# A conditioned residual block with a gathered layer norm: y begun a batch ahead, h read ahead of x^T, gathers issued later, batch 1's statistics taken before the nets

## What is computed

```python
h = ln(x, pw_g[path], pw_b[path]); h = ln(h, cp_g[cls], cp_b[cls])
t = ln(x, tm_g[cls], tm_b[cls]);   s = ln(x, ms_g[scale], ms_b[scale])
m, n, r = [x + mlp_ln(state_i) for the three states]     # one row per batch
cat = [w0*h, w1*t, w2*m, w3*n, w4*r, w5*s]               # w = softmax(aw)
out = x + ln(silu(cat @ W1 + b1) @ W2 + b2) * g + be
```

## Time and profile before

| | us |
|---|---|
| median of three runs (lowest, highest) | 998.59 (990.33, 999.7) |
| the profiled execution | 992.41 |
| its span, first to last instruction | 990.7 |
| PE busy in the span | 956.3 |
| DVE busy | 802.9 |
| POOL busy | 455.5 |
| PE idle for DVE's `ts_mult` (12 times) and `h_low` (8 times) | 12.3 and 7.1 |

### The profile page before, as it was taken

One profiled execution on the slowest core, in us unless ns is written; L12 is line 12 of the kernel. 1 busy time (PEld: TensorE's weight loads), 2 busy tenths in 40 slices (PEclk: granted clock), 3 DMA queues, 4 the chain that ended last, 5 costly groups with the idle time before them and its releaser, 6 DMA issues. The chain is left out here.

```text
span 990.7 us, 13506 instructions
## 1 busy us (share of the span) xinstructions
PE 956.3 (97%) x4196; PEld 773.7 (78%) x4196; DVE 802.9 (81%) x1183; ACT 271.4 (27%) x341; POOL 455.5 (46%) x619
## 2 busy tenths in 40 slices
PE   7999998999999999999999999999999999999997
PEld 6677877778877787887888888777877878787885
DVE  6887969788696878979787896978869697896965
ACT  4532232231322213223231322223132222313211
POOL 3335244445443554445455444545544355454322
PEclk9999999999999999999999999999999999999999
DMA  9956363847548465563847456384664838466362
GB/s 312 324 215 192 103 196 117 244 105 238 149 141 228 137 209 131 174 198 119 262 139 225 125 184 187 119 249 126 217 146 145 238 117 242 97 211 171 96 149 64
DMA packets 97425, 174.33 MB, mean 176 GB/s; under 512 B 10216, under 2 KB 48872, under 8 KB 93440
## 3 DMA queue, kind: packets, MB, share of 16 engines
q1 hardware_dynamic: 74432, 108.04, 33.8%
q0 software_dynamic: 22976, 66.07, 25.0%
HBM read 141.33 MB, written 32.75 MB: 176 GB/s over the span
## 5 line engine op out<-in xcount | busy, mean ns | idle before, releaser
L1440 PE MATMUL hid_ps<-cat_hi,w_hi 128*128 128x512 f32 x1008 | 394.1, 391 | 7.5 <-DVE cat_lo L961 7.1
L1441 PE MATMUL hid_ps<-cat_lo,w_hi 128*128 128x512 f32 x1008 | 392.5, 389 | 0.0
L1442 PE MATMUL hid_ps<-cat_hi,w_lo 128*128 128x512 f32 x1008 | 392.4, 389 | 0.0
L1440 PEld LDWEIGHTS hid_ps<-cat_hi,w_hi 128*128 128x128 f32 x1008 | 189.2, 188 | 53.3 <-DVE cat_lo L961 11.3
L1442 PEld LDWEIGHTS hid_ps<-cat_hi,w_lo 128*128 128x128 f32 x1008 | 189.2, 188 | 39.7
L1441 PEld LDWEIGHTS hid_ps<-cat_lo,w_hi 128*128 128x128 f32 x1008 | 189.3, 188 | 38.9
L555 POOL DMA_INDIRECT pw_rows<-cp,class_now x64 | 103.0, 1610 | 162.5 <-DVE y_sb L969 152.3
L734 ACT ACTIVATE cat_hi<-v_ring 128x1024 fp32r<-128x1024 f32 x64 | 67.9, 1062 | 335.5 <-DVE v_ring L951 335.4
L548 POOL DMA_INDIRECT pw_rows<-pw,path_now x64 | 75.5, 1179 | 83.6 <-DVE y_sb L994 71.4
L569 POOL DMA_DIRECT2D r_sb<-x x60 | 57.6, 959 | 108.0 <-DVE r_sb L1056 99.6
L1537 PE MATMUL o_ps<-w_hi,hid_hi 128*128 128x512 f32 x240 | 93.4, 389 | 0.0
(11 more groups left out here) (170 smaller groups left out, 1209.2 us busy)
## 6 DMA issues: line engine op xcount, KB each, us to landing
x_sb<-xp SPq DMA_DIRECT2D x16, 1024.0 KB, 4.8
out<-r_sb SPq DMA_DIRECT2D x64, 256.0 KB, 4.0
xc<-xT SPq DMA_DIRECT2D x15, 1024.0 KB, 10.2
h_turned<-y_sb SPq DMA_DIRECT2D x60, 256.0 KB, 6.4
r_sb<-x POOLq DMA_DIRECT2D x60, 256.0 KB, 5.4
v_ring<-h_turned SPq DMA_DIRECT2D x60, 256.0 KB, 4.1
stats_bc<-token_stats SPq DMA_DIRECT2D x30, 256.0 KB, 5.5
ids_sb<-ids SPq DMA_DIRECT2D x16, 256.0 KB, 5.8
```

The source lines that it names most:

```text
L1440: pe.matmul(acc, w1_hi[:, k, cols], hi, start=start, stop=False)
L1441: pe.matmul(acc, w1_hi[:, k, cols], lo, start=False, stop=False)
L1442: return pe.matmul(acc, w1_lo[:, k, cols], hi, start=False, stop=stop)
```

## The change

The matmuls and the vector instructions stay the same. What moves is their order.

On SP, `h_read(b, 0)` comes before `load_xT(b + 1)`:

```diff
-                if not by_pe(b):
+                if not first:
                     h_write(b)
+                    h_read(b, 0)
                 if not (first or last):
                     load_xT(b + 1)
-                if not by_pe(b):
-                    h_read(b, 0)
+                if not first:
                     h_read(b, 1)
-                if not first:
                     store(b - 1, 0)
```

On POOL, all four gathers of batch b + 1 stand together, behind `out_rstd(b - 1, 0)`, and all four class gathers stand ahead of `out_rstd(b - 1, 3)`; in the prologue all gathers of batch 1 and `x_rstd(1)` come ahead of `net_rstd`:

```diff
             def chunk(b, last=False):
-                if not (isinstance(b, int) and b == 1):
-                    for t in (2, 3):
-                        gather_class(b, t)
-                    for t in (2, 3):
-                        y_rstd(b, t)
+                y_rstd(b, 2)
+                y_rstd(b, 3)
+                out_rstd(b - 1, 0)
                 if not last:
                     path_ids(b + 1)
-                    gather(b + 1, 0)
-                    gather(b + 1, 1)
-                out_rstd(b - 1, 0)
-                if not last:
-                    gather(b + 1, 2)
-                    gather(b + 1, 3)
+                    for t in range(TT):
+                        gather(b + 1, t)
                     class_ids(b + 1)
```

On DVE, `y_mul` of all four tiles of batch b + 1 runs in batch b, ahead of `h_low(b, 1)`; its wait is now for the write of h (`h_out`) and no longer for `h_low`:

```diff
-                wait(dve, h_lo_done, 2 * b)
+                if isinstance(b, int) and b == 1:
+                    dve.wait_ge(filled, FT + 2)
+                elif not (isinstance(b, int) and b == 0):
+                    dve.wait_ge(h_out, 64 * (b - 1))
```

The new order of DVE's `chunk` (batch 1 has `w2_low` behind the second `hidden_low`, the last batch leaves out what serves b + 1):

```diff
+                y_add(b, 2)
+                ts_mult(b, 1)
+                y_add(b, 3)
+                y_norm(b, 0)
+                y_norm(b, 1)
+                ts_low(b, 1)
+                y_norm(b, 2)
+                y_norm(b, 3)
+                y_turn(b, 0)
+                ts_mult(b, 2)
+                y_turn(b, 1)
+                y_turn(b, 2)
+                y_turn(b, 3)
+                ts_low(b, 2)
...
+                out_stats(b - 1, 0, o_ps[:, 0, :])
...
+                out_sum(b - 1, 0)
+                ts_mult(b, 3)
```

More of the change, by code:

```diff
@@ L638, in chunk @@
                 add_x(b - 1, 2)
+                if not last:
+                    for t in range(TT):
+                        gather_class(b + 1, t)
                 out_rstd(b - 1, 3)
-                if not last:
-                    gather_class(b + 1, 0)
-                    gather_class(b + 1, 1)
                 add_x(b - 1, 3)
@@ L813, in chunk @@
                 hidden_high(b - 1, 1)
[L814 to L827, removed]
+                ts_high(b, 1)
+                for t in range(TT):
+                    y_hat(b, t)
+                ts_high(b, 2)
+                ts_high(b, 3)
                 h_high(b, 0)
+                h_high(b, 1)
                 if not last:
                     x_high(b + 1, 0)
-                h_high(b, 1)
-                if not last:
                     x_high(b + 1, 1)
@@ L1213, in first_chunk @@
                     y_norm(0, t)
[L1214 removed]
+                for t in range(TT):
+                    x_stats(1, t)
                 nets_stats()
                 h_low(0, 0)
+                w_low(13)
                 w_low(14)
                 w_low(15)
[L1219 to L1226 removed]
@@ L1227, in first_chunk @@
                 pack_first()
                 turn_stats(1)
+                h_low(0, 1)
+                class_rows()
+                nets_norm()
+                x_low(1, 0)
                 x_low(1, 1)
+                nets_weigh()
+                y_mul(1, 0)
+                y_mul(1, 1)
                 onehot_next(1)
-                for t in range(TT):
-                    y_mul(1, t)
+                centre(1)
+                scaled_next(1)
+                y_mul(1, 2)
+                y_mul(1, 3)
@@ L1233, in first_chunk, with chunk @@
                 y_add(1, 0)
                 add_b1()
-                scaled_next(1)
-                centre(1)
-                for t in range(1, TT):
-                    y_add(1, t)
-            def chunk(b, last=False):
-                if isinstance(b, int) and b == 1:
-                    ts_mult(b, 0)
-                    hidden_low(b - 1, 0)
-                    ts_low(b, 0)
-                    hidden_low(b - 1, 1)
+                y_add(1, 1)
+            def chunk(b, first=False, last=False):
+                ts_mult(b, 0)
+                hidden_low(b - 1, 0)
+                ts_low(b, 0)
+                hidden_low(b - 1, 1)
+                if first:
@@ new lines, in chunk @@
+                ts_low(b, 3)
+                out_stats(b - 1, 1, o_ps[:, 1, :])
+                out_sum(b - 1, 1)
+                h_low(b, 0)
+                out_stats(b - 1, 2, o_ps[:, 0, :])
+                if not last:
+                    turn_stats(b + 1)
+                out_sum(b - 1, 2)
+                if not last:
+                    for t in range(TT):
+                        y_mul(b + 1, t)
+                h_low(b, 1)
+                if not last:
+                    x_low(b + 1, 0)
+                    x_low(b + 1, 1)
```

135 lines of the change are left out of this document (24 added, 111 removed).

## The result

| | before | after |
|---|---|---|
| median of four runs each, us (lowest, highest) | 994.46 (986.27, 999.7) | 964.01 (963.75, 964.37) |
| ratio after/before, 95% interval | | 0.9701 (0.9623, 0.9779) |
| the profiled execution; its span | 992.41; 990.7 | 963.75; 962.0 |

The kernel is 3.0% faster, 4 us under the forecast of 968. The scatter of 13 us is gone too, as it would be if what varied was how late DVE came; no run tests that.

What follows compares the result with a forecast made beforehand. PE's matmuls were taken to bound the kernel, so only its idle time could go: 992.41 less 21.7 (loop), 1.7 and 0.95 (batch 1), 0.5 (batch 15) gave 967.5, called 968 us, range 964 to 972 at 0.70.

Steps and rivals of the forecast that it cites:

- y ended as counted: In each loop batch the last y_turn would end 16.8 us after ts_mult(b, 0) starts, where it was 21.15.
- When PE never waits: 57.34 us: PE's batch, bias to bias, without waits: 252 matmuls at 0.2275 us; 13 such periods against 767.13 us gave 21.7 us lost.
- the sum: The profiled execution less the predicted savings: 992.41 - 21.7 - 1.7 - 0.95 - 0.5 = 967.5 us.
- The wait of 3.4 goes: DVE's wait at scaled for the statistics would vanish: statistics at 46.2 to 48.2, scaled at 49.6 us after fill 0.
- I take 1.6 to 5: DVE's remaining waits per batch, from a possible 1.6 to 7.6 us, against 7.1 us of waiting before DVE sets the period.
- the slower rival: Late gathers at y_mul hold up h_low(b, 1) and PE's h pairs; 10 us above 998.59 takes 41/14 = 2.9 us more; chance 0.05.
- The floor is the write as it stands, 11.2: With h read ahead of x^T, the write of h still takes 11.2 us; half 0 is high-rounded from 30.5 to 34.2.
- Half 1 behind x^T: Half 1 of h lands by 41.6, 42.7 with ACT's rounding; DVE waits 0 to 2 us and ends before 47.8.
- Class gathers: Four on POOL ahead of out_rstd(b - 1, 3), 2.63 us each plus 0.3; DVE waits zero to 2 us, its 0.86 wait goes.
- The start of batch 1: Earlier statistics let fill 0 start at 86.5 us, where the bias matmul started at 87.45: 0.95 us saved.
- The rivals: Alternatives to the forecast: waits trade places, 972 to 988 us, 0.16; gain eaten, 988 to 1008, 0.09; slower, 0.05.
- A gain eaten whole: DVE's waits stay at 8.2 us in other places, time within 10 us of 998.59, needing three things at once; chance 0.09.

Runs made afterwards that it cites:

- Run 3: The changed kernel with the store of residual 0 on SP behind the spread of the statistics: 963.24 us, 0.9718 to the kernel before.
- run 4: The changed kernel with four more bn_stats per batch on DVE behind the last out_sum: 994.33 us, 1.0007 to the kernel before.
- Kernel 2: The changed kernel with the first two pathway gathers on POOL ahead of out_rstd(b - 1, 0), as before: 963.74 us, 0.9711 to the kernel before.
- run 6: The kernel before with y_norm of tiles 0 and 1 moved to the start of their own batch, behind hidden_low: 1000.62 us, 1.0075.
- run 7: The kernel before with h_read(b, 0) issued ahead of x^T of the next batch: 1038.48 us, 1.0453.
- run 8: The kernel before with h_read(b, 0) ahead of x^T and all four pathway gathers on POOL behind out_rstd(b - 1, 1): 1016.66 us, 1.0246.
- run 11: The changed kernel with batch 1's statistics behind the nets on DVE, and their root behind the nets' on POOL, as before: 974.69 us, 0.9813.
- run 1: The changed kernel with x^T of the next batch issued ahead of h_read(b, 0) again: 1003.25 us, 1.0107 to the kernel before.
- run 9: The kernel before with turn_stats(b + 1) ahead of h_low(b, 0) on DVE: 982.21 us, 0.9862.
- kernel 10: The kernel before with turn_stats ahead of h_low(b, 0) and the store of residual 0 behind the statistics' spread: 969.77 us, 0.9757.
- run 12: The changed kernel with two gathers early, residual 0's store behind the statistics' spread, and another order in DVE's prologue: 963.68 us, 0.9702.

## Why the prediction was right, and where it was not

*Its frame held.* PE set the time, its idle time was all there was to gain, and all of it in the loop went: 24.6 us. y ended as counted, 16.7 us after `ts_mult(b, 0)` in batch 9 (560.81 + 1.88 - 546.00) against 16.8, and DVE's own work is 50.3 us a batch, as predicted. But several of its steps failed, and that the time came out all the same is in part luck, as the waits below show.

*The floor was mis-sized.* "When PE never waits: 57.34 us" was read off a batch that PE was busy throughout. It holds a seam at fill 1, in the kernel before:

```profile
509.40 0.39 PE L1442 MATMUL hid_ps<-cat_hi,w_lo 128*128 128x512 f32 x1
509.69 0.73 PE L1420 MATMUL made_ps<-scaled,class_tab 128*128 128x512 f32 x2
510.26 0.40 PE L1440 MATMUL hid_ps<-cat_hi,w_hi 128*128 128x512 f32 x1
```

From start to start these are 0.29 and 0.57 us, where one matmul and two take 0.227 and 0.453: too short to be listed as a wait. The changed kernel's batches have 252 matmuls in 57.12 us, 0.22667 each. Thirteen times 0.22 is 2.9 of the 3.8 us that the profiled execution came below the sum; the start gave 0.8 more and the tail 0.2.

*"The wait of 3.4 goes" failed.* It stayed, 48.3 us in 14, since SP waits for the residual's store ahead of the statistics, and POOL adds that residual behind four gathers. The first gather and `add_x` of batch 9:

```profile
567.63 1.06 POOL L547 DMA_INDIRECT pw_rows<-pw,path_now  x1 [0.87 <-POOL path_now L528]
...
574.51 0.98 POOL L568 DMA_DIRECT2D r_sb<-x  x1 [0.77 <-POOL class_now L536]
```

The residual is added from 574.51 on and stored at 583.57, and the statistics follow at 583.97. The working had counted the gathers for their landing, not for what queues behind them on POOL, nor SP behind that. Run 3 shows it. It cost no time, as PE had nothing to wait for just the same.

*The waits that remain were mis-sized, and the margin with them.* "I take 1.6 to 5" against 7.1 that cost nothing. The waits of DVE other than for PE, added up from the brackets of its timeline over the 13 loop batches, are 6.4 us a batch: 3.3 for the statistics, put at nothing, 1.7 for `out_sum` 1 and 2, as counted, 0.7 for h, and 0.5 ahead of `ts_mult`. So under half a microsecond a batch was left, where the working had 2 to 5.5. As a sum the 7.1 us hold: in the profiled execution of run 4 the same waits are 6.9 and the work is 2.9 more, together 2.7 over the 7.1, and the batches from 2 on are 2.9 longer. What fails is to take waits for a reserve that shrinks when work is added. The margin of 41 us for the slower rival goes with it. Kernel 2 behaves as the prediction had it, with 3.3 us of such waits, and it is no faster: what the four late gathers took was the margin, not time.

*"The floor is the write as it stands, 11.2" failed.* It is 6.6 in the changed kernel, where the first gather is issued 4.9 us behind the write's start, 7.2 to 8.5 with two issued before the write, and 9.6 to 12.7 with two before it and two right at its start (runs 2, 6 and 7, last batches aside); 6.5 to 6.7 with the gathers 9 us behind (run 8). This is what the later gathers do; with y earlier as well, even two of them early are harmless.

*Half 1 behind x^T* came as said: DVE takes it at 42.3. *Class gathers* were priced at 2.63 each and took 1.09, 1.35, 0.95 and 0.96 in batch 9, but up to 3.64 in others; over the run their mean is 1.43, against 1.61 in the kernel before. No run settles what stretched the one in the earlier trace rows. So the inference of the Trainium skill ("SBUF — State Buffer", Who interferes with whom), against which the prediction set that row, is neither refuted nor borne out.

*The start of batch 1* gave 1.0 us at the bias and 1.5 at the fill, near 0.95. But the term hid what it rests on: with the new order of y, `batch_bias` stands behind `scaled` and `centre`, and without the early statistics the same place costs 10.7 us (run 11).

*The rivals.* None came, but x^T's order shows how near one was: one line swapped, and the changed kernel is slower than before (run 1). A gain eaten whole took one thing, x^T ahead of the read, and not the three at once that the prediction named.

What made the time fall is, as far as the runs go, the ring. In batch 9 its pieces were 38.3 + 9.3 + 10.8 = 58.5 us before (566.03, 604.36, 613.66, 624.49 in the earlier trace rows), over PE's 57.1, and are 34.7 + 14.6 + 7.5 = 56.8 now: the turn no longer stands behind a long wait for h, two `y_mul`, an `x_low` and two `y_norm` left the last piece, and the statistics' way took 5.3 us of it back. In the changed kernel the ring doesn't run over `turn_stats` itself, as the statistics lie ready for 3.3 us: it runs over POOL's gathers, the residual behind them and SP's store. Runs 9 and 10 get most of the gain from the turn of the statistics and SP's order by themselves, and run 4 shows that the changed kernel's loop has next to nothing to spare. The early y alone, with every gather and read as before, was not run, nor was a version of kernel 10 that also begins batch 1 early, so how much each part of the change gave is open.

## What to carry to other kernels

Look for the ring of dependences that comes back to the same instruction one batch later and add up its work and its transfers; an engine's idle time is no reserve for work that stands elsewhere in the ring (run 4). A move on one queue (h ahead of x^T) can be 4.5% slower alone and 4% faster in company, so price it with what is under way beside it: which transfers, and who stands behind the wait on the issuing engine. Take the floor from matmul spacing times count, not from the best period seen.

## What the runs showed of the hardware

PE's clock after idle time: in run 1 PE waited 2.05 to 2.61 us five times and 2.82 and 2.90 us once each, and behind these waits ran 8 and 14 matmuls at 0.43 us, the 1.2 GHz level, which cost some 1.7 and 3.0 us. The waits of 2.70 and 3.56 us in run 11 and of 3.56 in run 12 were followed by such matmuls too. The granted clock (the third figure from the end) shows it, in two windows of run 1, of which the first has the wait of 2.90 in it and the second one of 1.53:

```profile
326.10:389.20 63.10, 60.20 (x253) 49.26 (x252) 51.13 (x75) 15.69 (x18) 30.38 (x41) 0.95 0.56 164
389.20:448.20 59.00, 57.47 (x254) 47.23 (x253) 46.10 (x67) 15.70 (x18) 26.07 (x35) 1.00 0.58 172
```

But waits of 2.5 us in the kernel before, of 2.0 in run 7 and of 2.66 in the changed one's prologue left the matmuls at the 2.4 GHz level. So idle time of this length may cost about its own length again, and the length alone doesn't say whether.
